# Selection matmuls of a deformable convolution: two over the whole TensorE array in place of four over its quarters

## The reference

```python
x_proj = inputs @ w_in + b_in                                   # inputs = layernorm(x)
x1 = gelu(layernorm(depthwise_conv3x3(inputs)))
offset = (x1 @ w_off + b_off).reshape(B, H, W, G, K2, 2)
mask = softmax((x1 @ w_mask + b_mask).reshape(B, H, W, G, K2), axis=-1)
px, py = position of the tap + offset
out = sum over the 9 taps of bilinear_gather(x_proj, px, py) * mask   # zero outside of the image
x = x + out @ w_out + b_out
t = x + sum over the top 2 experts of weight * (gelu(norm(x) @ W1 + b1) @ W2 + b2)
```

## Time and profile before

| | us |
|---|---|
| median of 3 runs | 319.5 |
| lowest and highest run | 318.43, 329.28 |
| profiled execution, its own time | 320.6 |
| span of its trace | 318.8 |
| mean granted TensorE clock, share of 2.4 GHz | 0.925 |

### The profile page before, as it was taken

One profiled execution on the slowest core, in us unless ns is written; L12 is line 12 of the kernel. 1 busy time (PEld: TensorE's weight loads), 2 busy tenths in 40 slices (PEclk: granted clock), 3 DMA queues, 4 the chain that ended last, 5 costly groups with the idle time before them and its releaser, 6 DMA issues.

```text
span 318.8 us, 10339 instructions
## 1 busy us (share of the span) xinstructions
PE 294.8 (92%) x4248; PEld 176.8 (55%) x4248; DVE 226.7 (71%) x636; ACT 256.2 (80%) x494; POOL 116.5 (37%) x123
## 2 busy tenths in 40 slices
PE   7987999999999998999999999999599999999895
PEld 2553576445557653455568554455365666666563
DVE  6989778985757789559988749658936255378355
ACT  4798679888777999999788999997737997887473
POOL 5210161406042605031563450313743916248530
PEclk9999999755559999999999999999958999998999
DMA  6510000000000000000000000000000000000000
GB/s 143 116 33 2 3 3 2 3 2 0 2 2 3 3 3 2 0 4 1 2 19 4 3 2 1 2 2 2 8 10 3 2 3 10 2 2 4 8 2 19
DMA packets 5645, 3.50 MB, mean 11 GB/s; under 512 B 5073, under 2 KB 5278, under 8 KB 5534
## 3 DMA queue, kind: packets, MB, share of 16 engines
q1 hardware_dynamic: 5598, 2.84, 4.2%
HBM read 2.04 MB, written 0.52 MB: 8 GB/s over the span
## 4 chain that ended last, share of the span: by engine, by line
PE 64%; ACT 14%; DVE 12%; issue 6%; POOL 3%; DVEq 0%; ACTq 0%; POOLq 0%
PE zh_ps L1534 12%; PE ga_ps L1570 9%; PE ga_ps L1571 7%; PE zl_ps L1534 6%; ACT wk L1287 5%; PE m_ps L1656 4%; PE m_ps L1673 3%; ACT wk L1282 3%; PE m_ps L1454 2%; PE m_ps L1510 2%; PE m_ps L1640 2%; PE m_ps L1634 2%; PE m_ps L1642 2%; DVE wx L857 1%; ACT h_all L1311 1%
## 5 line engine op out<-in xcount | busy, mean ns | idle before, releaser
L1282 ACT ACTIVATE wk<-zh_ps 128x512 f16<-128x512 f32 x144 | 86.6, 601 | 32.9 <-PE zh_ps L1535 31.5
L869 DVE TENSOR_TENSOR prod<-ga_ps,wx 128x480 f32<-128x480 f32 x96 | 62.4, 653 | 53.8 <-PE ga_ps L1571 53.3
L1570 PEld LDWEIGHTS ga_ps<-v_all,wk 128*128 128x128 f16 x1152 | 69.0, 98 | 33.5 <-issue 26.7
L1287 ACT ACTIVATE wk<-zl_ps 128x512 f16<-128x512 f32 x144 | 86.3, 599 | 0.1
L1570 PE MATMUL ga_ps<-v_all,wk 128*128 128x40 f16 x1152 | 82.4, 184 | 1.3 <-DVE prod L869 0.5
L1571 PE MATMUL ga_ps<-v_all,wk 128*128 128x40 f16 x1152 | 80.7, 183 | 0.0
L558 POOL TENSOR_TENSOR prod<-prod 128x960 f32<-128x960 f32 (+1 forms) x20 | 36.8, 1841 | 105.5 <-DVE prod L869 105.5
L1571 PEld LDWEIGHTS ga_ps<-v_all,wk 128*128 128x128 f16 x1152 | 68.5, 99 | 2.6 <-issue 0.3
L1534 PE MATMUL zh_ps<-tab,sel_hi 64*64 64x512 f16 (+1 forms) x180 | 62.7, 381 | 3.2 <-ACT wk L1282 1.9
L1534 PE MATMUL zl_ps<-tab,sel_hi 64*64 64x512 f16 (+1 forms) x180 | 62.7, 381 | 3.1 <-ACT wk L1287 1.5
L1535 PE MATMUL zh_ps<-tab,sel_lo 64*64 64x512 f16 (+1 forms) x180 | 62.8, 381 | 0.0
(11 more groups left out here) (280 smaller groups left out, 558.4 us busy)
## 6 DMA issues: line engine op xcount, KB each, us to landing
h_all<-in_W SPq DMA_DIRECT2D x1, 512.0 KB
w_s<-in_W SPq DMA_DIRECT2D x1, 512.0 KB
x_tok<-in_x SPq DMA_DIRECT2D x1, 384.0 KB, 7.3
out_dram<-x_tok SPq DMA_DIRECT2D x6, 64.0 KB, 1.7
w_high<-w_high SPq DMA_DIRECT2D x1, 256.0 KB, 2.8
const<-in_table SPq DMA_DIRECT2D x1, 218.0 KB, 3.0
vec<-in_vectors SPq DMA_DIRECT2D x1, 132.5 KB
x_tok<-in_x SPq DMA_DIRECT2D x1, 128.0 KB, 2.3
```

The lines of the kernel that those rows point to most:

```text
L869: dve.tensor_tensor(prod[q % 2][:].rearrange("p k n -> p (k n)")[:, f * PB * NV:(f + 1) * PB * NV] .rearrange("p (n c l) -> p n c l", n=2 ...
L1282: act.activation(wk[n % WR][:, 0, :], zh_ps[:], ACT.Relu, scale=W_SCALE).then_inc(s_wkh, 1)
L1287: act.activation(wk[n % WR][:, 1, :], zl_ps[:], ACT.Relu, scale=W_SCALE).then_inc(s_wkl, 1)
L1570: pe.matmul(to, w, image[:, 1 + g, :], start=True, stop=False)
```

## The change

sel_hi and sel_lo become one tensor `sel`, 128 partitions x 2 groups x 9 taps x 128 columns. For group g it holds the old sel_hi in its own 64 columns and sel_lo in the other 64, in the partitions of the group; the 64 partitions of the other group are zero. The matmul takes all 128 partitions of `tab`, and one matmul of 128 rows and 128 columns gives what two of 64x64 gave. coef_lo and the last form of coef_hi become `coef`, 128 x 2 x 128, with zeros from a memset of POOL.

```diff
-        sel_hi = sb("sel_hi", [P, FW, KC], F16)
-        sel_lo = sb("sel_lo", [P, FW, KC], F16)
+        sel = sb("sel", [P, 2, FW, P], F16)
...
-        coef_lo = sb("coef_lo", [P, KC])
+        coef = sb("coef", [P, 2, P])
...
                 pool.wait_ge(s_selc, 1)
-                pool.tensor_tensor(sel_lo[:, 0:SEL_POOL, :], sel_own[:, 0:SEL_POOL].unsqueeze(2).to_broadcast([P, SEL_POOL, KC]),
-                                   coef_lo[:].unsqueeze(1).to_broadcast([P, SEL_POOL, KC]), ALU.mult).then_inc(s_sel, 1)
+                pool.tensor_tensor(sel[:, 1, 0:SEL_POOL, :], sel_own[:, 0:SEL_POOL].unsqueeze(2).to_broadcast([P, SEL_POOL, P]),
+                                   coef[:, 1, :].unsqueeze(1).to_broadcast([P, SEL_POOL, P]), ALU.mult).then_inc(s_sel, 1)
...
             pool.memset(xpad[:].bitcast(F32), 0.0)
+            pool.memset(coef[:], 0.0)
...
-                dve.tensor_scalar(coef_lo[:], sel_u[:], has(F_LOW), 1.0 / FINE, ALU.add, ALU.mult)
                 link(dve.scalar_tensor_tensor(coef_hi[:], sel_row[:], sel_col[:, 1:2], sel_u[:], ALU.mult, ALU.add))
-                dve.tensor_scalar(coef_hi[:], coef_hi[:], sel_col[:, 3:4], None, ALU.add).then_inc(s_selc, 1)
+                dve.wait_ge(s_zero, 1)
+                for g in range(2):
+                    own, other = (slice(i * KG, (i + 1) * KG) for i in (g, 1 - g))
+                    dve.tensor_scalar(coef[own, g, other], sel_u[own, :], sel_in[own, F_LOW:F_LOW + 1], 1.0 / FINE, ALU.add, ALU.mult)
+                    ins = dve.tensor_scalar(coef[own, g, own], coef_hi[own, :], sel_col[own, 3:4], None, ALU.add)
+                ins.then_inc(s_selc, 1)
...
-            dve.tensor_tensor(sel_hi[:], sel_own[:].unsqueeze(2).to_broadcast([P, FW, KC]),
-                              coef_hi[:].unsqueeze(1).to_broadcast([P, FW, KC]), ALU.mult).then_inc(s_sel, 1)
+            dve.tensor_tensor(sel[:, 0, :, :], sel_own[:].unsqueeze(2).to_broadcast([P, FW, P]),
+                              coef[:, 0, :].unsqueeze(1).to_broadcast([P, FW, P]), ALU.mult).then_inc(s_sel, 1)
...
-                ins = act.activation(sel_lo[:, f, :], coef_lo[:], ACT.Copy, scale=sel_own[:, f:f + 1])
+                ins = act.activation(sel[:, 1, f, :], coef[:, 1, :], ACT.Copy, scale=sel_own[:, f:f + 1])
...
                 q, k = n // K2, n % K2
-                own, other = (slice(i * KG, (i + 1) * KG) for i in (g, 1 - g))
-                pe.matmul(z_ps[g][own, to], sel_hi[own, k, :], tokens[own, q, :], start=True, stop=True)
-                return pe.matmul(z_ps[g][other, to], sel_lo[own, k, :], tokens[own, q, :], start=True, stop=True)
+                return pe.matmul(z_ps[g][:, to], sel[:, g, k, :], tokens[:, q, :], start=True, stop=True)
```

## The result

The kernel after takes 309.1 us (median of 4 runs, 308.6 to 310.0), the kernel before 322.3 in the same comparison (4 runs, 318.4 to 329.3). The ratio is 0.969 (95% interval 0.964 to 0.974), 3.1% faster; run again in another comparison (e8) it was 309.5 us with 0.967 (0.963 to 0.972). The ratios leave out runs that lay more than 1.5% above the fastest of their kernel, so they aren't the quotients of the medians. The time is also steadier: all ten runs lie within 1.5 us, where the kernel before spreads from 318.4 to 329.3 us.

A forecast was written before the change was run, and what follows sets the result against it. PE was taken as the bound, handing it to and fro with ACT. The sum 320.6 - 4.0 + 1.1 - 5.0 + 0.25 = 312.9 us, less 1.1 us from profiled execution to median, gave 311.8 us; range 307 to 315.

The forecast's parts named there:

- toll goes, columns double, clock stays up: Selection on PE: about 0.2 us standstill per tap vanishes, two 512-column passes replace side-by-side quarters, clock up between 60 and 95 us.
- What bounds: Whole kernel: PE, 92% busy and 64% of the last-ending chain, is the bound, handed to and fro with ACT.
- Free taps: Selection with both banks free: 0.44 us becomes 0.46; 57 such taps at the high clock cost +1.1 us.
- Handovers: Tap waiting for its second bank, followed by one with both free: 0.2 us saved each, 27 at high clock, taken as -4.0 us.
- Rows 7: Profile rows of a 512-column matmul over nearly the whole array, then the gather: follower 0.22 us later, so no standstill.
- The stretch at the lower clock: From 60 to 95 us, at 1.2 GHz before: clock up, ACT sets the pace, 30 us in place of 35, -5.0 us.
- clock up: 60 to 95 us: 512-column whole-array matmuls in every tap keep the clock up, as seen near such matmuls elsewhere; 7 in 10.
- The start: Before the first tap: more DVE work and a POOL memset add +0.25 us; POOL's longer product and ACT's copies stay hidden.
- Clock down: Rival: clock stays down between 60 and 95 us, only -1.2 us gained there; 315.7 us, chance 0.22.
- ACT takes over everywhere: Rival: each us PE gives back is spent in front of ACT's evictions; 319.5 us, chance 0.14.
- Toll stays: Rival at the step from selection to gather: concurrency lost, standstill stays, 0.22 us more per free tap; 328 us, chance 0.14.
- The correction of 1.1 us: Taken off the sum because the profiled execution, 320.6 us, lay above the runs' median of 319.5 us.

The follow-up runs named there:

- e8: Kernel after, unchanged, run again for a comparison on the same chip; 309.5 us, ratio 0.967 to before.
- e6: Kernel after, but whole-array selection in chunk 0 only, 64x64 quarters in chunks 1 to 3; 315.4 us, ratio 0.986 to before.
- e7: Kernel after, but 64x64 quarters in chunk 0, whole-array selection in chunks 1 to 3 only; 315.5 us, ratio 0.984 to before.
- e2: Kernel after, but each 128x128 selection matmul cut into two of 128 rows x 64 columns; 320.3 us, ratio 0.997 to before.
- e4: Kernel before, plus 21 matmuls of zeros behind gathers of chunk 0 from half step 15.5 on; 318.8 us, ratio 0.981.
- e9: Kernel after, but in chunks 0 to 2 the gather of two taps before stands between a tap's two selection matmuls; 319.3 us, ratio 1.000 to before.
- e5: Kernel after without the six keep_clock matmuls of zeros among the taps of chunk 0; 309.9 us, ratio 0.968 to before.
- e3: Kernel after, but each selection matmul takes only its group's 64 rows (64 rows x 128 columns); 322.3 us, ratio 1.001 to before.

## Why the prediction was right, and where its terms were off

The forecast was 311.8 us with the mechanism "toll goes, columns double, clock stays up"; measured 309.1.

- *What bounds.* Right. PE was the bound, to and fro with ACT; after the change ACT's evictions head the chain's list by line.
- *Free taps, +0.02 us each.* A free tap takes 0.45 us after (155.59 to 156.04) as before, where the sum had 0.46 against 0.44; the term of +1.1 us should have been near zero. Rows 7 did carry the price of the step to the gather.
- *Handovers, -4.0 us.* Waiting taps are where the gain lies, but the term was too small and its reason is only half right. From e6 to the kernel after, which differ in chunks 1 to 3 alone, the span falls by 4.8 us, 3.0 of them in taps 60 to 132; e7, with the whole array in these chunks alone, gains 1.6% or 5 us. With the +1.1 us of the free taps the sum had -2.9 us for both, so it was about 2 us short. In chunks 1 and 2 there are 71 steps from one tap's first selection matmul to the next tap's, and from e6 to after they lose 3.0 us: 1.4 us in the 20 from a waiting tap to a free one, 0.07 each, and 1.7 us in the 9 from a waiting tap to another waiting one, eight of them 0.20 to 0.22 us shorter. The prediction had 0.2 us for each of the first and 0.01 for each of the second. So the gain isn't made once for each handover; that the size came out near is in part luck. The page's issue time fell to 4.4 us (forecast: under 8), ACT's wait for zh_ps to 22.4 us (forecast: 18 to 24). (The three sorts of taps that were counted add up to 142, not 143; nothing hangs on it.)
- *The stretch at the lower clock, -5.0 us.* The clock stayed up, and taps 12 to 36 took 5.4 us less. Here the working had two slips that cancelled. ACT isn't 95% busy at full clock there but 32.06 / 35 = 92%, which makes 28.5 / 0.92 = 31.0 us and so 4.0 us in place of 5.0; the toll that goes in the same taps, 37.9 us with it (e2) against 36.6, makes up for it. e4 and e2 put the clock's own part at 3.1 and 4.2 us at least.
- *The ground for "clock up".* It was weaker than it read. The trace of before had two pairs of keep_clock's zeros inside the stretch at 1.2 GHz, and the clock did not rise:

```profile
62.62 1.02 PE L1617 MATMUL m_ps<-still 128*128 128x512 f16 x2
...
66.50 1.02 PE L1617 MATMUL m_ps<-still 128*128 128x512 f16 x2
```

  So a few such matmuls among quarters weren't enough here. With 21 of them the clock stayed up in two of four runs (e4), and with 512-column matmuls over all 128 rows in each tap it stayed up in after and e2. That is no warrant, though: e9 and e5 have the selection of after and their clock dipped in chunk 0, in e9 for some 10 us. The forecast of "up" was right at its 7 in 10, and its ground was an argument from neighbourhood, not a shown cause. What made the difference stays open: in after and e2 the two banks of a tap are computed one after the other and with the zero rows, in before and e3 mostly at the same time and without; no kernel separated the two.
- *The start, +0.25 us.* First eviction at 28.77 us in place of 28.54, +0.23. The DVE product took 1.36 us (forecast 1.4), POOL's 2.43 (2.5), positions began at 19.48 in place of 19.07, as forecast (+0.4):

```profile
18.21 1.36 DVE L1201 TENSOR_TENSOR sel<-sel_own,coef 128x1152 f16<-128x1152 f32 x1
18.25 2.43 POOL L582 TENSOR_TENSOR sel<-sel_own,coef 128x640 f16<-128x640 f32 x1 [2.69 <-DVE coef L688]
19.48 0.30 DVE L768 TENSOR_TENSOR py<-m_ps,base_v 128x144 f32<-128x144 f32 x1
```

- *The rivals.* "Clock down": no. "ACT takes over everywhere": in part, as the chain shows, but 3.1% came through first. "Toll stays": this kernel exists as e2, and it took 320.3 us, where the rival was priced at 328; the price had left out that the clock stays up there too.

The correction of 1.1 us from the profiled execution to the median of three was no help: over 25 and 11 later runs the kernel before had medians of 321.1 and 319.7 us, so which run is profiled moves the number by more than that.

The Trainium skill, "TensorEngine Tiling (Array Packing)", Tiling Modes, says under Key Properties that changing the mode drains the engine and changing only the tile doesn't. The runs agree: 0.11 to 0.12 us in and 0.32 to 0.34 out (0.22 of it columns) with 64x64, 128x64 and 64x128 parts, and nothing beyond the columns with the whole array. The speedup of up to 2x that it gives for a small dimension of 64 or less (Overview) held for the columns and was eaten here, because 512 columns are only 0.22 us of work between two changes.

## What to carry to other kernels

Packing small matmuls into parts of the array pays only if the work between two changes of part is long against the way in and out, here 0.2 us in all. Where it isn't, as with one 0.22 us pass between gathers here, weights padded with zeros and two passes over the whole array are as quick on PE, and quicker wherever the second bank had to be waited for. Before you price such a change, look at the granted clock of the stretch, since what the change does to the clock can be worth as much as the instructions themselves (e4: 1.9% by matmuls of zeros, in the runs in which the clock stayed up). And where PE waits for an eviction, another order of its work may only move the wait (e9).

## What the runs showed of the hardware that was not expected

- Halves and quarters cost the same toll. Ways out of 0.32 us were seen for 128x64 (150.47 to 150.79) and 64x128 (153.31 to 153.63), 0.33 to 0.34 for 64x64; ways in of 0.11 to 0.12 for all three. The kernel after still pays it elsewhere: the experts' second layer has 128x64 parts, and it starts 0.32 us behind a selection matmul whose columns take 0.22:

```profile
126.02 0.39 PE L1537 MATMUL zl_ps<-tab,sel 128*128 128x512 f16 x1
126.34 1.94 PE L1658 MATMUL m_ps<-h_all,w_s 128*64 128x512 f32 x8
```

- The clock stayed at 1.2 GHz for 34 us of a PE that was at work 97% of the time (34.08 of 35 us). In the kernel after PE is busy for 83% of the same stretch (29.09 of 35 us) with more matmuls (474 against 419) and keeps 2.4 GHz.
- The kernels with a steady clock have steady times: after 308.6 to 310.0 us over ten runs with mean clocks of 0.975 to 0.988, e2 319.3 to 320.5 over ten with 0.982 to 0.988, against 318.4 to 325.4 over 25 with 0.880 to 0.941 for the kernel before.
